# The first attention stage of an eight-stage kernel, written as one stream over its four batches

## The reference

```python
k = apply_rope(x @ Wk.T); v = x @ Wv.T            # one key/value head
q = apply_rope(einsum('btd,hkd->bhtk', x, Wq))    # two query heads, 128 wide
scores = einsum('bhtk,bsk->bhts', q, k) * HS ** (-0.5)
w = softmax(where(causal, scores, -inf), axis=-1)
out = einsum('bhts,bsk->bhtk', w, v)              # heads laid side by side
x = layernorm(x + out @ Wo.T)
```

## Time and profile before

| | us |
|---|---|
| median of three runs (lowest, highest) | 2108.05 (2103.53, 2110.74) |
| the profiled execution | 2110.27 |
| its span, first to last instruction | 2108.4 |
| share of the span: PE, DVE, ACT, POOL busy | 89%, 75%, 59%, 28% |
| first score; stores of y of the four batches | 26.07; 80.9, 147.35, 213.72, 279.50 |
| begin of the next stage | 283.7 |

### The profile page before, as it was taken

The page is one execution under the profiler, slowest core; times in us unless marked ns, Lnnn a source line. Parts: engine busy times, 40 slices in busy tenths (PEclk is TensorE's granted clock), DMA queues, the critical chain, the costliest instruction groups (busy, mean ns, idle before and its releaser), DMA issues. The chain is left out here.

```text
span 2108.4 us, 32001 instructions
## 1 busy us (share of the span) xinstructions
PE 1884.2 (89%) x10615; PEld 1281.7 (61%) x10624; DVE 1571.8 (75%) x3786; ACT 1249.2 (59%) x2554; POOL 597.4 (28%) x767
## 2 busy tenths in 40 slices
PE   7999979999599999669999999999799998995697
PEld 5667644444377777548888887888673444544342
DVE  4554547677447888659999999999533999997498
ACT  3335436656345555168888887887313768876465
POOL 2221216678302222200000000000000777777022
PEclk9999989999699999689999999999768999998799
DMA  2000020000200000000000000000310222222100
GB/s 91 30 30 0 30 88 11 15 6 11 89 22 11 21 11 11 6 20 2 6 16 1 6 16 6 2 7 16 132 62 2 53 59 63 63 68 67 48 26 26
DMA packets 34697, 65.80 MB, mean 31 GB/s; under 512 B 8406, under 2 KB 19743, under 8 KB 33783
## 3 DMA queue, kind: packets, MB, share of 16 engines
q1 hardware_dynamic: 26358, 47.16, 6.6%
q0 software_dynamic: 8192, 16.79, 3.1%
HBM read 51.34 MB, written 12.58 MB: 30 GB/s over the span
## 5 line engine op out<-in xcount | busy, mean ns | idle before, releaser
L2183 DVE SCALAR_TENSOR_TENSOR pk_level<-pk_sums,pk_least 128x1024 f32<-128x1024 f32 x256 | 322.3, 1279 | 22.8 <-ACT pk_sums L2092 21.6
L2092 ACT ACTIVATE pk_sums<-pk_sum 128x512 f32<-128x512 f32 x512 | 278.7, 602 | 94.5 <-PE pk_sum L2302 92.2
L2524 POOL DMA_INDIRECT tk_values<-top_keys_values,tk_index x256 | 241.8, 945 | 197.1 <-DVE tk_index L2744 119.4
L2310 PE MATMUL pk_weights<-product_keys_early_ident,pk_level 128*128 128x128 f32 x2048 | 269.5, 274 | 26.3 <-DVE pk_level L2183 24.3
L2310 PEld LDWEIGHTS pk_weights<-product_keys_early_ident,pk_level 128*128 128x128 f32 x2048 | 226.0, 141 | 52.9 <-DVE pk_level L2183 33.8
L2954 PE MATMUL tk_to_act<-tk_keys,tk_xT 128*128 128x512 f32 x512 | 236.0, 611 | 22.5 <-ACT tk_scores L2611 21.2
L2954 PEld LDWEIGHTS tk_to_act<-tk_keys,tk_xT 128*128 128x128 f32 x512 | 96.2, 195 | 144.2 <-issue 94.7
L1755 PEld LDWEIGHTS er_outs<-experts_early_w,er_hT 128*128 128x128 f32 x1024 | 134.0, 192 | 59.8 <-issue 56.4
L1165 PE MATMUL ml_outs<-experts_early_we,ml_xT 128*128 128x512 f32 x320 | 160.1, 628 | 3.5 <-DVE ml_r L1022 3.5
L2302 PE MATMUL pk_sum<-pk_lay_corners,pk_partsT 96*128 96x256 bf16 x1024 | 154.1, 272 | 0.9 <-ACT pk_sums L2092 0.9
L2742 DVE MAX8 tk_best<-tk_scores 128x8 f32<-128x4096 f32 x32 | 141.2, 4413 | 14.9 <-ACT tk_scores L2611 14.9
(11 more groups left out here) (437 smaller groups left out, 3700.0 us busy)
## 6 DMA issues: line engine op xcount, KB each, us to landing
tk_scores<-top_keys_compress SPq DMA_DIRECT2D x1, 4096.0 KB
tk_values<-top_keys_values,tk_index POOLq DMA_INDIRECT x256, 2.5
att_x_proj<-x_first SPq DMA_DIRECT2D x4, 512.0 KB, 5.3
att_x_res<-x_first SPq DMA_DIRECT2D x4, 512.0 KB, 4.3
x_after_attention<-att_y SPq DMA_DIRECT2D x4, 512.0 KB, 5.0
experts_early_w<-experts_w SPq DMA_DIRECT2D x2, 1024.0 KB
x_after_attention<-ml_y SPq DMA_DIRECT2D x8, 256.0 KB, 2.0
experts_ahead_x<-x_after_attention SPq DMA_DIRECT2D x8, 256.0 KB, 3.4
```

The lines of the kernel that those rows point to most:

```text
L2092: act.activation(sums[:, n % SUMS, half * HALF:(half + 1) * HALF], bank[:], ACT.Copy).then_inc(S.free.sem, 1)
L2183: dve.scalar_tensor_tensor(level[:, n % LEVELS, :], sums[:, n % SUMS, :], least[:, t % 2, h:h + 1], sums[:, n % SUMS, :], ALU.is_ge, ALU.m ...
L2310: ins = pe.matmul(weights[:, ch * P:(ch + 1) * P], level[:, n % LEVELS, ch * P:(ch + 1) * P], ident[:], is_transpose=True, start=h == 0 an ...
L2524: pool.indirect_dma_start(out=values[:, slot, k, :], out_offset=None, in_=c["values"], in_offset=bass.IndirectOffsetOnAxis(ap=index[slot][ ...
```

## The change

Only this stage and its weights are touched. The loops over batches become straight code: one stream of 32 units, n = 8b + u, and in iteration n each engine also does its part of the next batch's preparation, if there is one. Iterations -8 to -1 prepare batch 0 and do nothing else but the first score.

- x of all batches is loaded at the beginning into one buffer, behind the tables and ahead of the next stage's weights; it serves both projections and residual.
- Projections: one matmul for each tile with xT as stationary and the three weights side by side (384 columns), so tokens are on partitions. No swapped weights. VectorE turns with three multiplications, two of which read and write every second element; GpSimd adds 384 elements into `rotated` (two slots); TensorE transposes the three parts into A; ScalarE copies them into qT (with the scale) and kT. An addition waits for the transposes of two tiles before, a turn for the addition of two before.
- Wv and Wo are multiplied once on TensorE; values are x times that product, 256 wide (two heads), in two slots. The output projection and the copy before it go. Weighing has the transposed probabilities as stationary and the values of a head as moving, 128 columns a pass.
- The units' order stays: score of n+1, weighing of n-1, transposes of n, then the preparation: unit 0 transposes of x and values 0 and 1; unit 1 projections 0 to 2 and values 2 and 3; unit 2 projections 3 to 5, transposes of 0 and 1; unit 3 projections 6 and 7, transposes of 2 to 4; unit 4 transposes of 5 to 7.
- VectorE: maxima of n+1, residual of n-1, turns, normalisation of n-2. GpSimd: root of n-1, then the additions. ScalarE: exponentials of n+1, copies of n, then those of the preparation. Small buffers are four deep instead of two, y is two deep.

```diff
+        wqk = m.sb("wqk", [P, COLS]); wvT = m.sb("wvT", [P, P]); wo = m.sb("wo", [P, HEADS, P]); wvo = m.sb("wvo", [P, HEADS * P])
...
+        PROJECTED = {1: (0, 1, 2), 2: (3, 4, 5), 3: (6, 7)}
+        TURNED = {2: (0, 1), 3: (2, 3, 4), 4: (5, 6, 7)}
+        VALUED = {0: (0, 1), 1: (2, 3)}
...
+            return ([("xT", g) for g in range(HALVES)] if u == 0 else []) + [("qk", t) for t in PROJECTED.get(u, ())] + \
+                   [("v", g) for g in VALUED.get(u, ())] + [("qkT", t) for t in TURNED.get(u, ())]
...
-            sp.dma_start(x_proj[:], x_in[0]).then_inc(x_proj_in.sem, x_proj_in.unit)
+            sp.dma_start(x[:, 0], x_in[0]).then_inc(x_loaded[0], 16)
...
+            for b in range(1, B):
+                sp.dma_start(x[:, b], x_in[b]).then_inc(x_loaded[b], 16)
...
+            def add_turned(b, t):
+                q = b * TILES + t
+                pool.wait_ge(V.free.sem, taken_from_V("qk", b, t))
+                if q >= 2:
+                    pool.wait_ge(A.full.sem, made_for_A("qkT", *divmod(q - 2, TILES)))
+                pool.tensor_tensor(rotated[:, q % 2, :], turned[:, q % 2, 0].rearrange("p h d -> p (h d)"),
+                                   turned[:, q % 2, 1].rearrange("p h d -> p (h d)"), ALU.add).then_inc(rotated_ready, 1)
...
+            for n in range(-UNITS, ALL + 1):
+                if n >= 1:
+                    root(n - 1)
+                if n < ALL and prepared(n):
+                    b, u = prepared(n)
+                    for t in PROJECTED.get(u, ()):
+                        add_turned(b, t)
...
+            def take_qkT(b, t):
+                act.wait_ge(A.full.sem, A.to_take(0))
+                bank = A.take()
+                if b >= 2:
+                    act.wait_ge(scored, (b - 1) * UNITS * HEADS)
+                at = slice(t * P, (t + 1) * P)
+                act.activation(qT[:, b % 2, :, at], bank[:, 0:HEADS * P].rearrange("p (h n) -> p h n", h=HEADS),
+                               ACT.Copy, scale=float(P) ** -0.5)
+                act.activation(kT[:, b % 2, at], bank[:, HEADS * P:COLS], ACT.Copy).then_inc(A.free.sem, 1)
...
+            def turn(b, t):
+                q = b * TILES + t
+                dve.wait_ge(V.full.sem, V.to_take(0))
+                bank = V.take()
+                after(dve, rotated_ready, q - 1)
+                both = bank[:, 0:COLS].rearrange("p (h d) -> p h d", d=P)
+                dve.tensor_tensor(turned[:, q % 2, 0], both, spread(cos[:, t, :], 1, HEADS + 1), ALU.mult)
+                dve.tensor_tensor(turned[:, q % 2, 1, :, 0::2], both[:, :, 1::2], spread(sin[:, t, 0::2], 1, HEADS + 1), ALU.mult)
+                dve.tensor_tensor(turned[:, q % 2, 1, :, 1::2], both[:, :, 0::2], spread(sin[:, t, 1::2], 1, HEADS + 1),
+                                  ALU.mult).then_inc(V.free.sem, 1)
...
+            for n in range(-UNITS, ALL + 2):
+                if 0 <= n + 1 < ALL:
+                    maxes(n + 1)
+                if 1 <= n <= ALL:
+                    residual(n - 1)
+                if n < ALL and prepared(n):
+                    b, u = prepared(n)
+                    for t in PROJECTED.get(u, ()):
+                        turn(b, t)
+                if n >= 2:
+                    normalise(n - 2)
...
+            def project(b, t):
+                pe.wait_ge(A.free.sem, taken_from_A("xT", b, t // PER_HALF))
+                bank = claim_V()
+                pe.matmul(bank[:, 0:COLS], xT[:, t * P:(t + 1) * P], wqk[:], start=True, stop=True).then_inc(V.full.sem, 1)
+            def make_values(b, g):
+                pe.wait_ge(wvo_ready, 1)
+                pe.wait_ge(A.free.sem, taken_from_A("xT", b, 2 * g // PER_HALF))
+                bank = claim_A()
+                for i in range(2):
+                    t = 2 * g + i
+                    ins = pe.matmul(bank[:, i * HEADS * P:(i + 1) * HEADS * P], xT[:, t * P:(t + 1) * P], wvo[:], start=True, stop=True)
+                ins.then_inc(A.full.sem, 1)
+            def transpose_qk(b, t):
+                q = b * TILES + t
+                pe.wait_ge(rotated_ready, q + 1)
+                bank = claim_A()
+                for i in range(HEADS + 1):
+                    ins = pe.transpose(bank[:, i * P:(i + 1) * P], rotated[:, q % 2, i * P:(i + 1) * P], ident[:])
+                ins.then_inc(A.full.sem, 1)
...
+            def weigh_values(n):
...
+                for k in range(u + 1):
                     for h in range(HEADS):
+                        own = slice(h * P, (h + 1) * P)
+                        ins = pe.matmul(bank[:, own], probsT[:, n % 2, k, own], v[:, b % 2, k, own],
+                                        start=k == 0 and h == 0, stop=k == u and h == HEADS - 1)
+                ins.then_inc(V.full.sem, 1)
...
+            multiply_weights()
+            for n in range(-UNITS, ALL + 1):
+                if 0 <= n + 1 < ALL:
+                    if n + 1 == 0:
+                        pe.wait_ge(wvo_ready, 1)
+                    score(n + 1)
+                if n >= 1:
+                    weigh_values(n - 1)
+                if 0 <= n < ALL:
+                    transpose_probs(n)
+                if n < ALL and prepared(n):
+                    b, u = prepared(n)
+                    for what, i in in_turn(u):
+                        if what == "xT":
+                            transpose_x(b, i)
+                        if what == "qk":
+                            project(b, i)
+                        if what == "v":
+                            make_values(b, i)
+                        if what == "qkT":
+                            transpose_qk(b, i)
...
-        "wq": Wq.transpose(2, 0, 1), "wqr": np.stack([swap_pairs(w) for w in Wq]).transpose(2, 0, 1),
-        "wk": Wk.T, "wkr": swap_pairs(Wk).T, "wv": i["L0_attn_Wv"].T,
+        "wqk": np.concatenate([Wq[0], Wq[1], Wk], axis=0).T, "wvT": i["L0_attn_Wv"],
```

More of the change, by code:

```diff
@@ new lines, in take_probsT @@
+            def take_probsT(n, j):
+                blocks = min(2, n % UNITS + 1 - 2 * j)
+                act.wait_ge(A.full.sem, A.to_take(0))
+                bank = A.take()
+                if j == 0 and n >= 2:
+                    act.wait_ge(V.full.sem, made_for_V("out", n - 2))
+                act.activation(probsT[:, n % 2, 2 * j:2 * j + blocks, :].rearrange("p k n -> p (k n)"),
+                               bank[:, 0:blocks * HEADS * P], ACT.Copy).then_inc(A.free.sem, 1)
+            take_wvo()
@@ new lines, in maxes, with residual @@
+            def maxes(n):
+                keys = (n % UNITS + 1) * P
+                for h in range(HEADS):
+                    dve.wait_ge(scored, n * HEADS + h + 1)
+                    after(dve, exped, (n - KEPT + 1) * HEADS)
+                    dve.tensor_reduce(neg_max[:, n % KEPT, h:h + 1], scores[:, h, 0:keys], AX.X, ALU.max,
+                                      negate=True).then_inc(maxed, 1)
+            def residual(n):
+                b, u = divmod(n, UNITS)
+                s = n % KEPT
+                dve.wait_ge(exped, (n + 1) * HEADS)
+                steps.link(dve.reciprocal(inv_sum[:, s, :], row_sum[:, s, :]))
+                dve.wait_ge(V.full.sem, V.to_take(0))
+                bank = V.take()
+                if u == 0:
+                    dve.wait_ge(x_loaded[b], 16)
+                steps.link(dve.scalar_tensor_tensor(r1[:, s, :], bank[:, 0:P], inv_sum[:, s, 0:1],
+                                                    x[:, b, u, :], ALU.mult, ALU.add))
+                dve.scalar_tensor_tensor(r[:, s, :], bank[:, P:2 * P], inv_sum[:, s, 1:2], r1[:, s, :],
+                                         ALU.mult, ALU.add).then_inc(V.free.sem, 1)
+                dve.wait_ge(V.free.sem, taken_from_V("out", n))
+                norm_stats(steps, dve, r[:, s:s + 1, :], stats[:, s:s + 1, :],
+                           moments[:, s:s + 1, :]).then_inc(moments_ready, 1)
```

408 lines of the change are left out of this document (167 added, 241 removed).

## The result

| | before | after |
|---|---|---|
| median of ten runs each (lowest, highest) | 2110.53 (2103.30, 2111.48) | 2100.49 (2098.55, 2102.81) |
| the profiled execution | 2110.27 | 2100.19 |
| first score | 26.07 | 31.64 |
| a batch in the middle | 66.4 | 62.25 |
| end of the last y; begin of the next stage | 279.41; 283.71 | 270.33; 274.10 |

The ratio after to before is 0.9962, with a 95% interval of 0.9951 to 0.9972: 10 us faster, where 16.0 were forecast. The stage ends 9.6 us earlier by the profile, so the difference lies in this stage and nearly nothing of it behind. The runs are compared by their traces, and of these the one of the run warm alone is of a slow execution (2236.32 us, where its fastest took 2199.83); its batches take the same 62.24 us as those of the kernel after.

A forecast was written before the change was run, and what follows sets the result against it. TensorE's passes were taken to fill each batch but for some 10 us of waits. First score, batches and ending put the last y at 263.4 against 279.4: 2110.3 - 16.0 = 2094.3, less 2.2 to the median, 2092; range 2080 to 2106.

The forecast's parts named there:

- first score: End of the first batch's exposed preparation: forecast at 31.2 against 26.07 before, 5.1 us lost.
- the new wait: Additions wait for transposes queued behind projections that wait for turns: 2.4 us from turn 3 to 4 and 5 to 6.
- batch 0, to the tenth unit's score: From the first score: 1.4 us to the second score, then 57.9 for batch 0.
- two middle batches: Two steady batches, forecast at 61.4 us each against 66.4 before, 122.8 together.
- last batch to its last weighing: Batch that prepares nothing: units 0 to 7 and 0.4 of excess, 43.7 us, placing the last weighing at 257.0.
- from there to the last y's end: After the last weighing begins at 257.0: 3.5 + 0.3, then 2.6 us, last y ready at 263.4.
- the full clock in batch 0: Low clock was forecast only for the weights' product and first transposes; first to second score taken as 1.4 us.
- the allowance for what the reckoning leaves out: 0.5 us a batch added to the 60.9 of the iterations, gauged on one stretch reckoned at 7.5, traced at 7.71.
- batch 0 without the weighing of a batch before: Batch 0 taken as a steady batch less 3.5 us: 61.4 - 3.5 = 57.9.
- Rival 1: Chain of turn, addition and transpose costs half of the reckoning: 8.5 us more gain, 2083.5; chance 0.20.
- Rivals 2 and 3: VectorE's turn slower: strided halves at half rate, 2102, chance 0.18; all three multiplications at half rate, 2115, chance 0.07.
- Rival 4: TensorE's marked busy time is true work, only some 5 us idle a batch: about 2107; chance 0.10.

The follow-up runs named there:

- warm: Changed kernel plus 45 transposes whose result nobody reads, in TensorE's waits ahead of the first unit; ratio 0.9983 to the kernel before, last y ends at 268.51.
- slots4: Changed kernel with four places instead of two for the added projections, nothing else; ratio 0.9872 to the kernel before, last y ends at 256.33.
- spread4_again: Changed kernel with preparation spread over units 0 to 7 and four places, executed once more; 2073.00 us, ratio 0.9820 to the kernel before.
- spread4: Changed kernel with preparation spread over units 0 to 7 and four places for added projections; ratio 0.9858 to the kernel before, middle batch 56.81 us.
- order: Changed kernel, still two places, with each tile's transposes between the projections instead of behind them; ratio 0.9928 to the kernel before, last y ends at 257.48.
- spread: Changed kernel, two places, preparation spread over units 0 to 7, transposes a unit behind their projection; ratio 0.9843 to the kernel before.
- late4: Changed kernel with four places, two projections a unit in units 3 to 6, transposes a unit later; ratio 0.9878 to the kernel before, middle batch 59.30 us.
- few4: Changed kernel with four places, two projections a unit in units 0 to 3, transposes a unit later; ratio 0.9875 to the kernel before, middle batch 58.82 us.

## Why the prediction was half right

**The mechanism** of the new wait was right in each link; what the prediction lacked is the clock (below). Turn 1.13 (measured 1.08), addition 1.0 (1.00), turns 4 and 6 waiting 2.4 (2.60 each), turn 4 at 23.0 (23.27), turn 6 at 27.6 (27.95), first score at 31.2 (31.64). The iterations of a middle batch were predicted as 7.8, 7.3, 6.9, 9.4, 8.3, 7.0, 8.3, 5.9 and are 7.98, 7.20, 7.07, 9.42, 8.58, 7.26, 8.40, 6.35. Turn 0 at 15.0 (15.06) was luck in part: TensorE began at 8.44 instead of 9.1, and needed 6.6 us up to the turn instead of 5.9.

**The sizes** were off by 6.9 us up to the last y, 263.4 against 270.33, all in one direction:

| term | predicted | measured | off |
|---|---|---|---|
| first score | 31.2 | 31.64 | 0.4 |
| batch 0, to the tenth unit's score | 59.3 | 62.57 | 3.3 |
| two middle batches | 122.8 | 124.5 | 1.7 |
| last batch to its last weighing | 43.7 | 45.10 | 1.4 |
| from there to the last y's end | 6.4 | 6.52 | 0.1 |

Two steps of the prediction failed, and they make 5.7 of the 6.9: the full clock in batch 0 (1.5) and the allowance for what the reckoning leaves out (1.1 in batch 0, 1.7 in the middle, 1.4 in the last).

*Batch 0.* The first step that failed is "batch 0 without the weighing of a batch before": it took TensorE's clock as full from the first score on. I had taken from the earlier trace rows that the first passes run at the low clock, and had reckoned that TensorE would be idle in the preparation, but didn't put the two together. The column of the granted clock in the earlier trace rows says 1.00 for both windows and doesn't show it; the lengths of the same 512-column passes in the kernel before do, 2.07 us for the first two against 1.02 later:

```profile
12.08 2.07 PE L499 MATMUL att_to_dve<-att_xT,att_wq 128*128 128x512 f32 x2
...
15.90 1.02 PE L499 MATMUL att_to_dve<-att_xT,att_wqr 128*128 128x512 f32 x2
```

The run warm shows 1.5 of the 3.3 us to be this. Of the rest, 0.7 is the stretch up to the third unit's score (5.7 predicted, 6.42 in warm), 1.1 much the same small excess as in other batches.

*The middle and last batches.* The second step that failed is the allowance of 0.5 a batch for what the reckoning leaves out. It was too small: 0.85 more a batch, mostly in units 4 to 7, and 1.4 in the last one. I had gauged it on one stretch, which came out 0.2 of 7.7 us short, and had laid part of that on the output projection. Eight such stretches of 0.2 are 1.6, not 0.5; the middle batches took 1.35 (62.25 against the 60.9 of the iterations). What the excess of each unit consists of no run has parted, so its cause stays open. Weighing itself isn't the cause: 32 passes span 3.65 us, (3.65 - 0.19)/31 = 0.112 each, where 0.111 was assumed.

*Behind the stage.* The next stage begins 3.8 us after the last y instead of 4.3, and the rest of the kernel is 0.5 us shorter by the profiled executions; these give back 1.0 of the 6.9, and 10.1 of the forecast 16.0 remain. The forecast of 2092 took off another 2.2, because the profiled execution lay above the median of three runs; the median of ten is 2110.53, right at it.

**The rivals.** Rival 1 (the chain costs half) fell at the start, where each of the two stalls is 2.60 and slots4 gains 5.2 in all (4.8 reckoned). In the batches it fell too, as units 3 and 4 took 9.42 and 8.58 us. But not all of their gap is the chain: with four places they still take 7.46 and 8.10, where the reckoning had 6.8 and 6.6 of work, so of 4.3 us reckoned the places give back 2.4. Rivals 2 and 3 fell with the 0.35 us of the strided halves. Rival 4 had 2107, 6.5 us off, nearer than 2092 (8.5 off), but for a wrong reason: marked busy time isn't TensorE's true work. For the same instructions of a batch it is 56.82 us in the kernel after and 55.37 in spread4_again, and spread4's batch of 56.81 is shorter than the 61 of before less the 3.6 us of passes that went. What the change leaves idle it leaves so by its order, not because nothing was idle.

**What the range meant.** 2080 to 2106 held 2100.49. The gain of 0.38% stands just over the 0.3% line.

**Where the gain went.** Of the 4.15 us that a middle batch gained, the fewer passes on TensorE account for 3.6 by the prediction's count and the stream for the rest, though the kernel before had some 10 us of idleness. Waits of 6.2 us in the units with the preparation stand where the kernel before had those of its separate preparation, and at the start they cost 5.6 us of the first score. The runs order and slots4 return most of the second and a part of the first, spread all but 0.8.

## What to carry to other kernels

When a later iteration's preparation is folded into a stream, spread it thinly, with the consumer of each handed-on buffer in the iteration behind its producer; where that can't be, put the step that frees a buffer ahead of the one that needs it in the same engine's order, or deepen the buffer. To see what a fill costs, take from the trace the same iterations without it (here those of the last batch), and compare the difference with the passes of the fill alone: what is over is waiting, and the iteration tells where. Behind a dependent opening that leaves TensorE half idle, look at the granted clock before you take full speed for the first microseconds.

## What the hardware showed that I had not expected

- Behind the stretch in which TensorE was half idle (busy 1.00 of 2.00 us from 28 to 30), it ran at 1.2 GHz until 37 us, in the first units of the stage; three weight loads took 0.50 us there against 0.31, and filler transposes removed it.
- VectorE reads every second fp32 element out of PSUM and writes every second one to SBUF, with a table spread over three heads as second operand, at the rate of contiguous ones: 192 elements in 0.35 us, 384 in 0.56.
- TensorE takes the preparation beside units of four to eight blocks of keys as cheaply as beside units of one to five (late4 against few4, within 0.5 us a batch): that a unit of few keys has gaps in it doesn't make it the better host of two projections. One projection and one fill of values in unit 1 of spread4 did cost less than their passes, 0.96 us for 1.46.
